# One transfer of 8 KB a partition for each head's position scores, in place of two of 4 KB

## The chip, the cores and the metric

The kernel runs on one core of a Trainium2 chip. The metric is the device time of one execution in microseconds, the median of several runs. The numbers of the profile come from one execution that the hardware profiler recorded.

## What is computed

The input is 32 batches of 512 tokens with 256 channels. A layer norm gives xn. To x are added an attention with relative positions over xn and a mixture of experts over xn. What matters here is the attention, with 16 heads of 16 channels:

```python
content_score = einsum('bhsp,bhtp->bhst', q + u, k)
pos_score = einsum('bhsp,htp->bhst', q + v, pos)
pos_score = _relative_shift(pos_score)      # pad one column in front, reshape (s, s+1) -> (s+1, s), drop the first row
score = (content_score + pos_score) / sqrt(P)
weights = softmax(score, axis=-1)
out = einsum('bhst,bhtp->bhsp', weights, val)
```

There are 32 x 16 = 512 heads, each with 512 x 512 position scores in fp32, 1 MB.

## The kernel before

The kernel has two phases. The attention phase first normalises all batches and then goes through the 512 heads; the expert phase (`ffn_phase`) follows, and begins when the attention phase has ended.

The relative shift of a head is done by memory. A partition holds four query rows. PE computes the position scores of a head into PSUM (`position`, L980), two query tiles at a time. ACT copies these two tiles into a ring of NW = 4 heads, `xo`, with a zero column in front of each row (`x_evacuate`, L604); two copies make a head, and each adds 1 to the semaphore `x_out`. SP writes the ring to the scratch tensor `xs_d` in DRAM as 512 rows of 513 words (`write_x`, L406), and reads the same memory back as rows of 512 words from word 512 on (`read_x`, L416) into `shifted`, which has NX = 8 slots. That is the shifted matrix. Each write and each read is done in two transfers, of rows 0 to 1 and rows 2 to 3 of every partition. Since a partition's four rows lie next to each other, on both sides of each transfer, a transfer of two rows has 4104 or 4096 bytes in one piece per partition, and one of four rows would have 8208 or 8192.

DVE adds the content scores, which PE computes (`content`, L991), to the shifted positions and keeps the least of each row (`add`, L765), then subtracts that least (`subtract_least`, L772). PE turns the result (L1012, L1013), ACT takes the exponential (L612), PE multiplies by the values (L1028). DVE works on head kk, PE and ACT on the positions of head kk + 5 (LEAD = 5).

SP's program is unrolled and strictly in order. In step kk it takes, for half 0 and then half 1: write head kk + 4, read head kk + 2. The waits in it:

- a write waits for the read of the head that had its DRAM slot 8 heads ago (`x_shifted`), and for the ACT copy of its own half (`x_out`);
- a read waits for the whole write of its head, made two steps earlier (`x_written`), and for the slot in `shifted` to be free (`t_full`);
- every fourth step `store_o` issues 4 transfers of 32 KB (L425) and 4 of 2 KB (L428) of finished output; every 16th step a batch's xt is loaded (L368).

ACT waits for `x_written` before it copies into a ring entry again, and DVE waits for `x_shifted` of a head, both halves, before its first addition (L762).

Of the kernel before, what the change touches and what calls it, by code (L numbers as in the profile page):

```python
# [18 lines left out]
B = 32  # L19
S = 512  # L20
TT = S // P
H = 16
# [26 lines left out]
def wait_alone(eng, sem, value):  # L49

    wait(eng, sem, value)
    if not isinstance(value, int):
        eng.nop(nofuse=True)
# [86 lines left out]
def attention_phase(nc, x, gate_w, w, w1, w2, consts, xn_d, xt_d, xs_d, att_d, sums_d, shared):  # L140
# [7 lines left out]
    LEAD = 5  # L148
    BEHIND = 2
    LAG = 2  # L150
    NX = 8
    NW = 4
    ND = 5
    BH = 2 * H
# [6 lines left out]
    with ExitStack() as ctx:  # L161
# [11 lines left out]
        shifted = m.sb("shifted", [P, NX, TT, S])  # L173
# [127 lines left out]
        x_out = m.sem("x_out")  # L301
# [48 lines left out]
        with nc.Block() as block:  # L350

            @block.sync
            def _(sp):
# [42 lines left out]
                        load_xt(0)  # L396
                store_xt(B - 1)

                def write_x(i, kk, half):

                    slot, turn = of_slot(kk)
                    if half == 0:
                        wait_alone(sp, x_shifted[slot], (i * (BH // NX) + turn) * 32)
                    rows = slice(2 * half, 2 * half + 2)
                    wait_alone(sp, x_out, (i * BH + kk) * 2 + half + 1)
                    sp.dma_start(xs_d[slot].rearrange("(p t c) -> p t c", t=TT, c=S + 1)[:, rows], xo[:, kk % NW, rows]).then_inc(x_written[slot], 16)  # L406

                def read_x(i, kk, half):

                    slot, turn = of_slot(kk)  # L410
                    if half == 0:
                        wait_alone(sp, x_written[slot], (i * (BH // NX) + turn + 1) * 32)

                        wait_alone(sp, t_full, (i * BH + kk - NX + 1) * TT)
                    rows = slice(2 * half, 2 * half + 2)
                    sp.dma_start(shifted[:, slot, rows], xs_d[slot][S:S + S * S].rearrange("(p t c) -> p t c", t=TT, c=S)[:, rows]  # L416
                                 ).then_inc(x_shifted[slot], 16)

                def store_o(i, q):

# [12 lines left out]
                for k in range(LEAD - 1):  # L433
                    if k == LEAD - 1 - BEHIND + 1:
                        for n in range(NS):
                            sp.wait_ge(xn_stored[n], 16 * (B // NS))
                            sp.wait_ge(xt_stored[n], 16 * (B // NS))
                    for half in range(2):
                        write_x(0, k, half)
                        if k >= BEHIND:  # L440
                            read_x(0, k - BEHIND, half)
                load_xt(1)

                def body(i):
                    first = isinstance(i, int) and i == 0
                    last = isinstance(i, int) and i == ITERS - 1
                    for kk in range(BH):
                        for half in range(2):
                            if not (last and kk + LEAD - 1 >= BH):
                                write_x(i, kk + LEAD - 1, half)  # L450
                            if not (last and kk + LEAD - 1 - BEHIND >= BH):
                                read_x(i, kk + LEAD - 1 - BEHIND, half)
                        if kk % H == 4 and not last:
                            load_xt(i * 2 + 2 + kk // H)
                        if kk % QH == 0 and not (first and kk < 2 * QH):
                            store_o(i, kk // QH - 2)
                        if last and kk == BH - 2:

                            for k in range(NX):
                                sp.wait_ge(x_written[k], B * H // NX * 32)  # L460
                            load_first(sp, w1, 0, w1s).then_inc(shared.w1_in, 16)
                            load_second(sp, w2, 0, w2s).then_inc(shared.w2_in, 16)

# [80 lines left out]
            def _(act):  # L544
# [53 lines left out]
                def x_evacuate(i, kk, half):  # L598

                    if half == 0 and not (isinstance(i, int) and i * BH + kk < NW):  # L600
                        slot, turn = of_slot(kk - NW)
                        act.wait_ge(x_written[slot], (i * (BH // NX) + turn + 1) * 32)
                    act.wait_ge(x_full, (i * BH + kk) * 2 + half + 1)
                    act.activation(xo[:, kk % NW, 2 * half:2 * half + 2, 1:S + 1], xp[:, :, :], ACT.Copy).then_inc(x_out, 1)  # L604

# [79 lines left out]
            def _(dve):  # L685
# [72 lines left out]
                def add(i, kk, t):  # L758

                    n = i * BH + kk  # L760
                    if t == 0:
                        slot, turn = of_slot(kk)  # L762
                        wait_alone(dve, x_shifted[slot], (i * (BH // NX) + turn + 1) * 32)
                    wait_alone(dve, s_full, n * TT + t + 1)
                    dve.tensor_tensor_reduce(out=shifted[:, kk % NX, t], in0=sp_[:, t % 2], in1=shifted[:, kk % NX, t], scale=-0.25,  # L765
                                             scalar=-NEG, op0=ALU.add, op1=ALU.min,
                                             accum_out=mn[:, kk % NX, t:t + 1]).then_inc(added, 1)
# [895 lines left out]
```

## Time and profile before

| | before |
|---|---|
| time, median of 3 runs | 4691.83 us (4685.78 to 4698.15) |
| profiled execution | 4698.8 us, span 4697.0 us |
| PE busy | 4317.0 us, 92% of the span |
| DVE busy | 3394.8 us, 72% |
| ACT busy | 3201.7 us, 68% |
| POOL busy | 1263.8 us, 27% |
| moved by DMA | 1391.15 MB, mean 296 GB/s |

Busy shares are averages over two phases with different limits: the heads are written and read from 160 to 3047 us, and the experts follow. Where time is lost is read from the waits of a stage and from the share of the 16 DMA engines in it. The profile's DMA share of a stretch is the time of the packets in it over 16 engines; as the records of neighbouring packets overlap a little, it can stand slightly above 1. A PE that is busy isn't PE at its peak, since matmuls are pipelined and their ends are modelled.

### The profile page before, as it was taken

The numbers are of one execution on the slowest core, as the hardware profiler recorded it, in microseconds if no ns is written. First come the engines' busy times: TensorE is split into PE (matmuls) and PEld (weight loads), VectorE is DVE, ScalarE is ACT, GpSimd is POOL, SyncE is SP. The second block draws the span as 40 slices with busy tenths as digits, with TensorE's granted clock in tenths as the row PEclk, the third lists the DMA queues.
The fourth block names the chain that finished last, engine by engine and source line by source line (L and its number), as shares of the span: only waits on it lengthen the run. The fifth ranks groups of instructions, "written<-read, shape, count | busy, mean of one in ns | idle before, by whom it ended". The sixth has DMA issues, their size and how long they took to land. (4 is left out here: it accounts for less than half of the span.)

```text
span 4697.0 us, 121317 instructions
## 1 busy us (share of the span) xinstructions
PE 4317.0 (92%) x48308; PEld 3333.7 (71%) x48308; DVE 3394.8 (72%) x8088; ACT 3201.7 (68%) x4124; POOL 1263.8 (27%) x905
## 2 busy tenths in 40 slices
PE   7899999999989999989998998889999999999997
PEld 3466666666666666666666666668888888888886
DVE  7688888888888888888888787755665666544455
ACT  2588888888888888888888888744444444444454
POOL 0111111111111111111111111125556666544443
PEclk9899999999999999999999999989999999999998
DMA  8999999999999999999999999972555555433259
GB/s 320 342 379 389 394 386 393 388 384 392 389 389 384 388 396 389 388 396 382 390 389 387 391 393 388 360 253 53 133 137 124 136 125 136 107 56 87 47 171 313
DMA packets 467836, 1391.15 MB, mean 296 GB/s; under 512 B 59216, under 2 KB 136656, under 8 KB 467024
## 3 DMA queue, kind: packets, MB, share of 16 engines
q1 hardware_dynamic: 418128, 1316.25, 74.1%
q0 software_dynamic: 49152, 67.14, 8.4%
q8 instruction: 391, 6.41, 0.5%
q14 instruction: 165, 1.35, 0.1%
HBM read 708.93 MB, written 674.23 MB: 294 GB/s over the span
## 5 line engine op out<-in xcount | busy, mean ns | idle before, releaser
L765 DVE CUSTOM_DVE_ANT_0 att_shifted<-att_quad,att_shifted 128x512 f32<-128x512 f32 x2048 | 1351.8, 686 | 507.4 <-PE att_quad L991 256.2
L604 ACT ACTIVATE ring<-att_quad 128x1024 f32<-128x1024 f32 x1024 | 1050.5, 1026 | 229.9 <-PE att_quad L980 205.2
L612 ACT ACTIVATE att_pt<-att_tp 128x1024 f32<-128x1024 f32 x1024 | 1047.7, 1023 | 17.9 <-PE att_tp L1013 13.0
L772 DVE TENSOR_SCALAR att_shifted<-att_shifted,att_mn 128x512 f32<-128x512 f32 x2048 | 1024.6, 542 | 0.0
L991 PE MATMUL att_quad<-att_kd,att_qd 64*128 64x512 f32 x2048 | 879.8, 462 | 149.2 <-DVE att_mn L765 134.6
L980 PE MATMUL att_quad<-att_pos,att_qd 64*128 64x512 f32 x2048 | 849.8, 445 | 91.4 <-ACT ring L604 84.1
L1420 ACT ACTIVATE ffn_hp<-ffn_up 128x512 fp32r<-128x512 f32 x512 | 306.2, 598 | 855.4 <-PE ffn_up L1601 818.4
L1506 DVE TENSOR_TENSOR ffn_hp<-ring,ffn_hp 128x512 fp32r<-128x512 f32 x512 | 440.4, 860 | 589.4 <-ACT ring L1422 528.8
L1012 PEld LDWEIGHTS att_tp<-ident,att_shifted 64*128 64x128 f32 x8192 | 669.6, 141 | 189.2 <-DVE att_shifted L772 109.9
L1601 PE MATMUL ffn_up<-ffn_xp,ffn_w1p 128*128 128x512 f32 x3072 | 796.1, 395 | 2.8 <-DVE ffn_xp L1449 2.8
L1012 PE MATMUL att_tp<-ident,att_shifted 64*128 64x64 f32 x8192 | 754.8, 229 | 43.1 <-ACT att_pt L612 32.8
L1013 PE MATMUL att_tp<-ident,att_shifted 64*128 64x64 f32 x8192 | 762.4, 230 | 2.5 <-issue 2.5
L1559 PE MATMUL ffn_yp<-ffn_w2p,ffn_hp 128*128 128x512 f32 x2048 | 745.5, 398 | 8.7 <-DVE ring L1465 6.9
L1013 PEld LDWEIGHTS att_tp<-ident,att_shifted 64*128 64x128 f32 x8192 | 669.3, 141 | 41.8 <-issue 6.1
L1601 PEld LDWEIGHTS ffn_up<-ffn_xp,ffn_w1p 128*128 128x128 f32 x3072 | 543.4, 189 | 115.9 <-DVE ffn_xp L1449 3.2
L991 PEld LDWEIGHTS att_quad<-att_kd,att_qd 64*128 64x128 f32 x2048 | 377.4, 190 | 334.3 <-DVE att_mn L765 217.9
L1351 POOL DMA_INDIRECT ffn_d<-ring,picks x256 | 432.0, 1688 | 634.8 <-DVE ring L1465 618.5
L1028 PE MATMUL att_op<-att_pt,att_val 128*17 128x128 f32 x16384 | 588.1, 286 | 8.3 <-issue 7.7
L1561 PE MATMUL ffn_yp<-ffn_w2p,ffn_hp 128*128 128x256 f32 x2048 | 573.7, 280 | 0.0
L980 PEld LDWEIGHTS att_quad<-att_pos,att_qd 64*128 64x128 f32 x2048 | 364.5, 190 | 199.5 <-issue 169.2
L499 POOL CAST att_kc<-att_qn 128x512 fp32r<-128x512 f32 x64 | 41.5, 648 | 1584.9 <-PE att_mp L910 1572.8
L1028 PEld LDWEIGHTS att_op<-att_pt,att_val 128*17 128x17 f32 x16384 | 422.5, 101 | 57.5 <-issue 10.0
(132 smaller groups left out, 5249.9 us busy)
## 6 DMA issues: line engine op xcount, KB each, us to landing
xs_d<-ring SPq DMA_DIRECT2D x1024, 513.0 KB, 8.7
att_shifted<-xs_d SPq DMA_DIRECT2D x1024, 512.0 KB, 8.8
att_shifted<-in_L_attn_x_dram SPq DMA_DIRECT2D x32, 512.0 KB, 6.6
xn_d<-att_shifted SPq DMA_DIRECT2D x32, 512.0 KB, 5.9
xt_d<-att_shifted SPq DMA_DIRECT2D x32, 512.0 KB, 7.2
gathered<-xt_d SPq DMA_DIRECT2D x32, 512.0 KB, 10.0
att_d<-att_osb SPq DMA_DIRECT2D x512, 32.0 KB
ring<-in_L_ffn_w_dram SPq DMA_DIRECT2D x16, 1024.0 KB
```

The source lines that it names most:

```text
L604: act.activation(xo[:, kk % NW, 2 * half:2 * half + 2, 1:S + 1], xp[:, :, :], ACT.Copy).then_inc(x_out, 1)
L612: act.activation(turned_keys(n, half), tp[:, :, :].rearrange("p r (k n) -> p k r n", k=2 * TT), ACT.Exp, scale=-1.0).then_inc(t_out, 1)
L765: dve.tensor_tensor_reduce(out=shifted[:, kk % NX, t], in0=sp_[:, t % 2], in1=shifted[:, kk % NX, t], scale=-0.25, scalar=-NEG, op0=ALU.ad ...
L772: dve.tensor_scalar(shifted[:, kk % NX, t], shifted[:, kk % NX, t], mn[:, kk % NX, t:t + 1], None, ALU.subtract).then_inc(lowered, 1)
L980: ins = pe.matmul(xp[:, t % 2, :], qd[rows, n // GH % ND, t * P:(t + 1) * P], pos[rows, kk // GH % NG8, :], start=True, stop=True)
L991: pe.matmul(sp_[:, t % 2, :], qd[rows, n // GH % ND, t * P:(t + 1) * P], kd[rows, kk // GH % 2, :], start=True, stop=True).then_inc(s_full, 1)
L1012: low = pe.transpose(tp[:, 0, at], shifted[0:ROWS, kk % NX, t, keys], ident[0:ROWS, 0:ROWS])
L1013: high = pe.transpose(tp[:, 1, at], shifted[ROWS:P, kk % NX, t, keys], ident[ROWS:P, ROWS:P])
L1028: ins = pe.matmul(op[32 * t:32 * t + HD + 1, kk % QH * P:(kk % QH + 1) * P], val[:, kk // H % 2, c, kk % H, :], pt[:, of_keys(n, c), t * P ...
L1559: pe.matmul(yp[:, k % 2, :], hp[:, g % 2, 0, f, tok], w2p[:, f].rearrange("p w d -> p (w d)"), start=(f == 0), stop=False)
L1561: ins = pe.matmul(yp[:, k % 2, 0:D], hp[:, g % 2, 1, f, tok], w2p[:, f, 0], start=False, stop=(f == FC - 1))
L1601: ins = pe.matmul(up[:, f % 4, :], w1p[:, wi, c, f * P:(f + 1) * P], xp[:, g % 2, xi, c, :], start=(s == 0 and c == 0), stop=(s == 2 and c ...
```

## The change

`write_x` and `read_x` lose their argument `half`. A head is written by one transfer of all four rows of a partition, once both ACT copies are done, and read by one. SP's order in step kk is now: write head kk + 4, read head kk + 2. The semaphores `x_written` and `x_shifted` go up by 16 a head in place of 32, and all that wait for them are adapted. The bytes, the buffers, the distances between heads and the other engines' programs are as before.

```diff
-                def write_x(i, kk, half):
+                def write_x(i, kk):
 
                     slot, turn = of_slot(kk)
-                    if half == 0:
-                        wait_alone(sp, x_shifted[slot], (i * (BH // NX) + turn) * 32)
-                    rows = slice(2 * half, 2 * half + 2)
-                    wait_alone(sp, x_out, (i * BH + kk) * 2 + half + 1)
-                    sp.dma_start(xs_d[slot].rearrange("(p t c) -> p t c", t=TT, c=S + 1)[:, rows], xo[:, kk % NW, rows]).then_inc(x_written[slot], 16)
-
-                def read_x(i, kk, half):
+                    wait_alone(sp, x_shifted[slot], (i * (BH // NX) + turn) * 16)
+                    wait_alone(sp, x_out, (i * BH + kk) * 2 + 2)
+                    sp.dma_start(xs_d[slot].rearrange("(p t c) -> p t c", t=TT, c=S + 1), xo[:, kk % NW]).then_inc(x_written[slot], 16)
+
+                def read_x(i, kk):
 
                     slot, turn = of_slot(kk)
-                    if half == 0:
-                        wait_alone(sp, x_written[slot], (i * (BH // NX) + turn + 1) * 32)
-
-                        wait_alone(sp, t_full, (i * BH + kk - NX + 1) * TT)
-                    rows = slice(2 * half, 2 * half + 2)
-                    sp.dma_start(shifted[:, slot, rows], xs_d[slot][S:S + S * S].rearrange("(p t c) -> p t c", t=TT, c=S)[:, rows]
-                                 ).then_inc(x_shifted[slot], 16)
+                    wait_alone(sp, x_written[slot], (i * (BH // NX) + turn + 1) * 16)
+
+                    wait_alone(sp, t_full, (i * BH + kk - NX + 1) * TT)
+                    sp.dma_start(shifted[:, slot], xs_d[slot][S:S + S * S].rearrange("(p t c) -> p t c", t=TT, c=S)).then_inc(x_shifted[slot], 16)
...
-                        for half in range(2):
-                            if not (last and kk + LEAD - 1 >= BH):
-                                write_x(i, kk + LEAD - 1, half)
-                            if not (last and kk + LEAD - 1 - BEHIND >= BH):
-                                read_x(i, kk + LEAD - 1 - BEHIND, half)
+                        if not (last and kk + LEAD - 1 >= BH):
+                            write_x(i, kk + LEAD - 1)
+                        if not (last and kk + LEAD - 1 - BEHIND >= BH):
+                            read_x(i, kk + LEAD - 1 - BEHIND)
```

## Rows read from the trace of the kernel before

**Rows 1.** The page: DMA share and GB/s in 40 slices of the span, SP's queue.

```profile
DMA  8999999999999999999999999972555555433259
GB/s 320 342 379 389 394 386 393 388 384 392 389 389 384 388 396 389 388 396 382 390 389 387 391 393 388 360 253 53 133 137 124 136 125 136 107 56 87 47 171 313
...
q1 hardware_dynamic: 418128, 1316.25, 74.1%
```

**Rows 2.** The page: issues of the positions' transfers, count, KB each, us to landing.

```profile
xs_d<-ring SPq DMA_DIRECT2D x1024, 513.0 KB, 8.7
att_shifted<-xs_d SPq DMA_DIRECT2D x1024, 512.0 KB, 8.8
```

**Rows 3.** Stages: busy time of each engine, granted clock, DMA share and rate.

```profile
core 0: us, PE busy (x) PEld busy (x) DVE busy (x) ACT busy (x) POOL busy (x), PEclk, DMA share, GB/s
...
1000.00:1500.00 500.00, 452.18 (x6858) 334.02 (x6858) 414.89 (x1122) 424.54 (x491) 71.77 (x56) 0.97 1.01 389
```

**Rows 4.** Waits of the whole span, the last two SP's own.

```profile
engine line waited for: us in total, times, longest us
...
DVE att_shifted L765 <- PE att_quad L991: 256.2, 376, 2.8
DVE att_shifted L765 <- DMA att_shifted<-xs_d: 236.7, 276, 2.3
...
SPq L406 <- ACT ring L604: 448.2, 386, 9.7
...
SPq L416 <- DMA xs_d<-ring: 284.2, 241, 3.4
```

**Rows 5.** The queues in 2064 to 2070, 1518 to 1521, 2034 to 2036 us.

```profile
DMA packets 675, 2.47 MB, mean 412 GB/s; under 512 B 73, under 2 KB 73, under 8 KB 674
...
q1 hardware_dynamic: 674, 2.46, 102.3%
...
DMA packets 539, 0.97 MB, mean 323 GB/s; under 512 B 99, under 2 KB 335, under 8 KB 538
...
q1 hardware_dynamic: 538, 0.95, 85.2%
...
DMA packets 418, 0.71 MB, mean 354 GB/s; under 512 B 80, under 2 KB 269, under 8 KB 418
...
q1 hardware_dynamic: 418, 0.71, 102.5%
```

**Rows 6.** The sums' load in SP's timeline, and the queue from 3079 to 3081 us.

```profile
3076.62 0.35 SPq L1254 DMA_DIRECT2D ffn_heads<-sums_d  x1
...
DMA packets 97, 0.74 MB, mean 369 GB/s; under 512 B 5, under 2 KB 5, under 8 KB 9
...
q1 hardware_dynamic: 97, 0.74, 100.8%
```

**Rows 7.** SP's timeline around a quad's stores: start, duration, line, transfer.

```profile
1514.75 0.43 SPq L416 DMA_DIRECT2D att_shifted<-xs_d  x1
1515.22 2.23 SPq L425 DMA_DIRECT2D att_d<-att_osb  x4
1517.49 2.39 SPq L428 DMA_DIRECT2D sums_d<-att_osb  x4
1519.97 0.39 SPq L406 DMA_DIRECT2D xs_d<-ring  x1
1520.46 0.38 SPq L416 DMA_DIRECT2D att_shifted<-xs_d  x1
1520.89 0.78 SPq L406 DMA_DIRECT2D xs_d<-ring  x1
1521.71 0.51 SPq L416 DMA_DIRECT2D att_shifted<-xs_d  x1
...
1525.02 0.32 SPq L406 DMA_DIRECT2D xs_d<-ring  x1
...
1527.66 0.32 SPq L406 DMA_DIRECT2D xs_d<-ring  x1
...
1530.16 0.32 SPq L406 DMA_DIRECT2D xs_d<-ring  x1
```

**Rows 8.** Line L406, the writes: from issue to landing.

```profile
DMA to landing us min/median/max: 3.3/8.7/10.9
```

More of the change, by code:

```diff
@@ L437, in _ @@
                             sp.wait_ge(xt_stored[n], 16 * (B // NS))
-                    for half in range(2):
-                        write_x(0, k, half)
-                        if k >= BEHIND:
-                            read_x(0, k - BEHIND, half)
+                    write_x(0, k)
+                    if k >= BEHIND:
+                        read_x(0, k - BEHIND)
                 load_xt(1)
@@ L447, in body @@
                     for kk in range(BH):
-                        for half in range(2):
-                            if not (last and kk + LEAD - 1 >= BH):
-                                write_x(i, kk + LEAD - 1, half)
-                            if not (last and kk + LEAD - 1 - BEHIND >= BH):
-                                read_x(i, kk + LEAD - 1 - BEHIND, half)
+                        if not (last and kk + LEAD - 1 >= BH):
+                            write_x(i, kk + LEAD - 1)
+                        if not (last and kk + LEAD - 1 - BEHIND >= BH):
+                            read_x(i, kk + LEAD - 1 - BEHIND)
                         if kk % H == 4 and not last:
@@ L459, in body @@
                             for k in range(NX):
-                                sp.wait_ge(x_written[k], B * H // NX * 32)
+                                sp.wait_ge(x_written[k], B * H // NX * 16)
                             load_first(sp, w1, 0, w1s).then_inc(shared.w1_in, 16)
@@ L601, in x_evacuate @@
                         slot, turn = of_slot(kk - NW)
-                        act.wait_ge(x_written[slot], (i * (BH // NX) + turn + 1) * 32)
+                        act.wait_ge(x_written[slot], (i * (BH // NX) + turn + 1) * 16)
                     act.wait_ge(x_full, (i * BH + kk) * 2 + half + 1)
@@ L762, in add @@
                         slot, turn = of_slot(kk)
-                        wait_alone(dve, x_shifted[slot], (i * (BH // NX) + turn + 1) * 32)
+                        wait_alone(dve, x_shifted[slot], (i * (BH // NX) + turn + 1) * 16)
                     wait_alone(dve, s_full, n * TT + t + 1)
```

## The prediction

> **What bounds the kernel now.** The page comes first. Its slices show two stages: up to about 3050 us DMA stands at 9 in every slice and moves 340 to 396 GB/s; behind that it falls to 40 to 140 GB/s for most of the rest [rows 1]. The change touches the first stage only. The 2048 half transfers of the positions [rows 2] carry 2048 x 512.5 KB, 1075 of the 1316 MB of SP's queue [rows 1].
>
> Next the stage table: from 1000 to 1500 us PE is busy 452, ACT 425 and DVE 415 of 500 us, the clock is granted at 0.97, and the DMA engines have a share of 1.01 at 389 GB/s [rows 3]. (A share above 1 says that the times of neighbouring packets overlap a little in the records.) So DMA has no room left; PE, ACT and DVE have 10, 15 and 17%.
>
> The waits say the same from the other side [rows 4]. DVE waits 236.7 us for a shifted head to land, in 276 of 512 heads, and 256.2 us for PE's content scores. SP waits 284.2 us for a write to land before it may read it back. PE's waits on DVE follow from these. So the loop is held by the DMA engines, with PE near behind. Full DMA engines mean that the time of a head is the work that those engines have for it: cut the work per head, and the loop gets shorter, until PE is next.
>
> **What a transfer costs on the engines.** The change leaves the bytes as they are and halves the number of packets, so I need the fixed cost of a packet. Three short stretches of the queue view give it [rows 5]. The first holds big transfers alone: 674 packets, 2.46 MB, 102.3% of 16 engines x 6 us = 98.2 us of packet time. The second holds many small ones: 538 packets, 0.95 MB, 85.2% of 48 us = 40.9 us. With time = n x o + bytes x b, the second scaled by 2.46 / 0.95 = 2.589 is 1393 packets and 105.9 us for the same bytes; the difference is 719 packets for 7.7 us, so o = 10.7 ns. The third (418 packets, 0.71 MB, 102.5% of 32 us = 32.8 us), scaled by 3.465, gives 774 packets for 15.4 us, o = 19.9 ns. The two differ by 9 ns, so I take 1.5 to 20 ns as bounds and 10.7 as the value: a wait inside a packet can only make o look larger.
>
> In the first stretch 73 packets are under 512 B and 601 are not, 8.2 to 1: each half transfer is 128 packets of 4 KB (one a partition) and 16 small closing ones.
>
> **The change, part by part.**
>
> 1. *Half the packets.* 2048 transfers of 144 packets become 1024 of 144, if 8 KB of a partition go in one packet. That they can is shown by the one transfer of before with 8 KB a partition, the sums' load at 3076.62 us: its stretch has 97 packets of which 9 are under 8 KB [rows 6]. 147,456 packets fewer, 9216 on each of 16 engines, x 10.7 ns = 98.6 us. It counts only where the engines are full: heads are moved from slice 2 to slice 26, and 23 of these 25 stand at 379 GB/s or more [rows 1], so 0.92 x 98.6 = 91 us. By the bounds: 13 to 169 us (1.5 and 20 ns).
>
> 2. *The first half of a write waits for the second.* A write now waits for both ACT copies of its head. Where no stores lie between, write halves go out at 1525.02, 1527.66 and 1530.16, 2.5 us apart [rows 7]. What is queued behind the waiting SP: the read of two heads earlier, and every fourth head the 8 small stores. Before, the read's first half went ahead of that wait, but DVE starts a head only when both halves have landed, so its last byte is issued at the same moment as before. The engines lose nothing as long as they have over 3 us of work queued at that time. From issue to landing a half transfer takes 8.7 us in the median [rows 8], and carries 1.3 us of work at 411 GB/s; the shortest, 3.3 us, is one with next to nothing ahead of it. So 5 us or more lie ahead in the median, which covers the wait: cost nothing. If that cover were gone it would be up to 1.3 us a head.
>
> 3. *The write is whole before the read of its turn.* On the engines the order was write half, read half, write half, read half; now write, then read. A write lands one half transfer (1.3 us) sooner relative to what is queued, and it is the write two heads ago for which SP waits 284.2 us before reading [rows 4]. That wait shrinks. I book nothing, since the engines were not idle during it.
>
> 4. *SP's issue.* Two issues a head in place of four, 0.32 us each when nothing is in the way. Every fourth head SP issues the stores of a quad, 1515.22 to 1519.88, and no large transfer goes out [rows 7]; then it catches up with issues of 0.4 to 0.8 us each, one behind the other. The engines pause after that: the q1 share of 85.2% over 3 us is a pause of 0.44 us [rows 5]. 128 such groups make at most 56 us. With whole transfers SP hands over twice the bytes an issue, so part of this may be won; I put it in the range, not in the sum. The waits' thresholds (16 in place of 32) cost nothing: the same number of waits, or fewer.
>
> 5. *What is late next.* The 91 us are 0.18 us of a head's 5.59 us (two issues of each kind a head, 1024 in all over 2870 us). DVE's landing waits are 0.46 us a head, so more is there than is taken. PE at 452 of 500 us still has room for a period shorter by 3.2%.
>
> Sum: 4697.0 us span plus 1.8 around it is 4698.8 us for the profiled execution; less 91 is 4608. That execution is 7 us above the median of the three runs, so against the median: 4601 us.
>
> **A rule of the notes that speaks against it.** The Trainium skill (DMA: Bandwidth & Descriptors, "Why small descriptors are slow (HBM only)") puts the fixed overhead at about 3 cycles a packet and holds joining to be worth it only at 256 B or less. With the 850 MHz that the page gives for the fabric that would be an estimate of 3.5 ns a packet, 9216 x 3.5 = 32 us, a time near 4660. The stretches above gave 10.7 and 19.9 ns, but they are few.
>
> **The rivals.**
>
> *B, the packet's fixed cost is small, or PE takes over at once.* At the low end of my bounds, 1.5 to 4 ns, part 1 is worth 13 to 34 us: 4658 to 4679, take 4670. The same time results if PE gives only a third of what DMA frees: DVE waits for PE more than for DMA [rows 4]. Against it: the engines show shares of 1.00 and more nearly throughout.
>
> *C, slower: the held first half starves the engines.* Place: the head behind a quad's stores, where the queue has run down. If the engines stand for one half transfer there, 1.3 us x 128 groups = 166 us, less the 91 us: +75, 4767 us. It decides from the point where less than about 3 us of work is queued when a first half becomes ready. For it: the 3.3 us shortest landing and the pauses in [rows 5]. Against: after the stores both halves are ready already, as the four issues from 1519.97 on without a gap show [rows 7].
>
> *D, slower: 8 KB packets take longer.* The stretch with the 8 KB load has 88 large packets and 9 others in 100.8% of 32 us, 32.3 us; all of it laid on the large ones is up to 367 ns each [rows 6]. In the plain stretch two 4 KB packets take 2 x 98.2 / 601 = 327 ns with their closing packets. If 367 held, 40 ns x 8192 large packets an engine = +328 us, 5020 us; the point from which it loses is 327 ns. I give this little, because that stretch holds the start of an idle queue, with the first packets' latency in it.
>
> *E, the change doesn't do what it says: the 8208 B rows of the write are cut into a large packet and a remainder.* Then only the reads have fewer packets: half of part 1, -46 us, 4646 us.
>
> **How the numbers follow.** A, my sum: 0.57, with its own range 4570 to 4640 (10.7 ns, give or take a third, and a part of the pauses). A with the pauses gone or a packet cost of 20 ns, some 4545 us: 0.07. B 0.14, C 0.10, D 0.05, E 0.07. A measurement of this kernel tells 0.3%, 14 us, from no change. Faster: A, its better case, E and about a third of B, 0.75; same: the rest of B, 0.10; slower: C and D, 0.15. The range runs from 4550 to 4690: it leaves out C and D (0.15) and about 0.05 at the low end.
>
> **What would show it.** Step 1: packets of q1 down by 147,456 to some 271,000, and plain stretches at 420 GB/s or more in place of 410. Step 2: no new pauses of DMA between quads, DVE's landing waits below 236.7 us; if they grow while the DMA share drops below 0.97, C is right. Step 3: SP's waits for written heads well below 284.2 us. Step 4: shares after the stores above 85%. Step 5: PE's busy share in the stage up from 0.90 to about 0.93. Wrong would be the sum if plain stretches stay at 410 GB/s (B or D), or if they rise and the period of a head doesn't fall below 5.5 us (PE next).

## The result, and the profile after

The changed kernel takes 4848.65 us (median of 4 runs, 4837.81 to 4869.45), the kernel before 4688.81 us on the same chip: a ratio of 1.034, 95% interval 1.032 to 1.036. It is slower by 160 us, where 90 us less was forecast. The profiled execution has a span of 4867.6 us.

| | before | after |
|---|---|---|
| span of the profiled execution | 4697.0 us | 4867.6 us |
| packets of SP's queue | 418128 | 270672 |
| DMA rate, 1000 to 1500 us | 389 GB/s | 361 GB/s |
| PE's granted clock, same stretch | 0.97 | 0.94 |
| DVE waits for a shifted head | 236.7 us | 339.8 us |

The page of the kernel after, in the form of [rows 1] and [rows 2]:

```profile
DMA  9899999999999999999999999984445555433259
GB/s 331 319 364 362 350 378 370 370 364 354 361 370 371 357 374 380 357 359 374 372 362 365 371 365 368 369 325 127 111 114 140 136 125 138 115 63 84 45 158 314
...
q1 hardware_dynamic: 270672, 1316.18, 74.9%
...
xs_d<-ring SPq DMA_DIRECT2D x512, 1026.0 KB, 8.5
att_shifted<-xs_d SPq DMA_DIRECT2D x512, 1024.0 KB, 10.6
```

The queue has exactly the 147,456 packets fewer that were forecast, for the same bytes, and yet its share of the span is no smaller. In the stage of the heads the slices stand at 350 to 380 GB/s where they stood at 379 to 396, and the stage lasts longer by that. The stage behind it is as it was. (The granted clock of PE goes along with this and doesn't look like its cause: PE is busy for less of the stretch, 437 us in place of 452, though its clock is lower.) The table of stages, to be held against [rows 3], and the waits of the whole span, against [rows 4] (SP's own last):

```profile
1000.00:1500.00 500.00, 436.81 (x6413) 321.36 (x6408) 388.90 (x1046) 395.81 (x458) 65.81 (x52) 0.94 1.00 361
...
DVE att_shifted L758 <- DMA att_shifted<-xs_d: 339.8, 301, 5.0
...
DVE att_shifted L758 <- PE att_quad L984: 322.5, 369, 3.2
...
SPq L46 <- ACT ring L597: 1783.5, 398, 9.8
```

SP's wait for the landing of a write, 284.2 us before, is down to 2.6 us. In its place SP stands 1783.5 us in the wait for both ACT copies (L46 is the helper `wait_alone`). Before, its waits for ACT copies were 448.2 us [rows 4] and, counted at the same helper, 349.3:

```profile
SPq L46 <- ACT ring L604: 349.3, 262, 3.9
```

The DMA share still reads 1.00 while the rate fell by 7%: the engines are counted busy with packets that move fewer bytes in the same time, as if they stood still for a part of it. Over the whole span this can be put in numbers. The share of q1, SP's queue, times the span is the time that its packets took on each engine: 74.1% of 4697.0 us is 3481 us before, 74.9% of 4867.6 us is 3646 us after. A third fewer packets for the same bytes took 165 us more, and what is left of the span grew only from 1216 to 1222 us. So the changed kernel isn't longer because its engines are idle more; its packets are slower.

Where packets stand still is seen in 1 us windows (columns as in [rows 3]: the last two are DMA share and GB/s), with SP's issues of that time:

```profile
1500.10 0.32 SPq L404 DMA_DIRECT2D xs_d<-ring  x1
1500.51 0.38 SPq L412 DMA_DIRECT2D att_shifted<-xs_d  x1
1505.28 0.32 SPq L404 DMA_DIRECT2D xs_d<-ring  x1
1505.69 0.38 SPq L412 DMA_DIRECT2D att_shifted<-xs_d  x1
1506.12 2.31 SPq L420 DMA_DIRECT2D att_d<-att_osb  x4
...
1505.00:1506.00 1.00, 1.00 (x6) 0.66 (x4) 0.59 (x1) 1.00 (x2) 0.00 (x0) 1.00 1.02 419
1506.00:1507.00 1.00, 1.00 (x15) 0.71 (x16) 1.00 (x5) 0.81 (x2) 0.00 (x0) 1.00 1.14 320
1507.00:1508.00 1.00, 1.00 (x42) 0.93 (x40) 1.00 (x2) 0.98 (x2) 0.00 (x0) 1.00 0.89 262
1508.00:1509.00 1.00, 1.00 (x20) 0.70 (x9) 1.00 (x5) 0.95 (x2) 0.00 (x0) 1.00 0.96 402
1509.00:1510.00 1.00, 1.00 (x20) 0.90 (x18) 1.00 (x3) 0.85 (x2) 0.81 (x1) 1.00 1.05 443
```

The engines are at 419 GB/s, drop to 320 and 262 for 2 us with shares of 1.14 and 0.89, and come back. A quad's stores are issued from 1506.12 on and may have a part in this one, but it returns about once a head, after each whole write: 324 and 321 GB/s from 1512 to 1514 us, and, where no store is near, 246 and 254 from 1500 to 1502 and 295 from 1518 to 1519. The plain stretch of before from 2064 to 2070 us stayed at 394 to 422 GB/s in each microsecond, 412 in the mean [rows 5].

### The profile page after: what moved, and what is told of

It is laid out like the page before. It is cut to its first block and busy times, and to the rows that moved or that the text cites. A ratio compares the mean times of both kernels' runs of the same rounds, so it can differ in the third digit from the quotient of the medians.

```text
span 4867.6 us, 120293 instructions
## 1 busy us (share of the span) xinstructions
PE 4397.3 (90%) x48308; PEld 3383.3 (70%) x48308; DVE 3408.2 (70%) x8088; ACT 3203.3 (66%) x4124; POOL 1243.2 (26%) x905
## 3 DMA queue, kind: packets, MB, share of 16 engines
q1 hardware_dynamic: 270672, 1316.18, 74.9%
## 5 line engine op out<-in xcount | busy, mean ns | idle before, releaser
L758 DVE CUSTOM_DVE_ANT_0 att_shifted<-att_quad,att_shifted 128x512 f32<-128x512 f32 x2048 | 1353.3, 685 | 669.3 <-DMA att_shifted<-xs_d 339.8
L984 PE MATMUL att_quad<-att_kd,att_qd 64*128 64x512 f32 x2048 | 903.5, 472 | 248.9 <-DVE att_mn L758 234.5
L973 PE MATMUL att_quad<-att_pos,att_qd 64*128 64x512 f32 x2048 | 882.6, 457 | 86.5 <-ACT ring L597 79.5
L1499 DVE TENSOR_TENSOR ffn_hp<-ring,ffn_hp 128x512 fp32r<-128x512 f32 x512 | 452.4, 884 | 571.3 <-ACT ring L1415 571.2
L1005 PE MATMUL att_tp<-ident,att_shifted 64*128 64x64 f32 x8192 | 774.9, 233 | 41.1 <-ACT att_pt L605 28.2
L1005 PEld LDWEIGHTS att_tp<-ident,att_shifted 64*128 64x128 f32 x8192 | 690.9, 144 | 171.5 <-DVE att_shifted L765 90.9
L1006 PE MATMUL att_tp<-ident,att_shifted 64*128 64x64 f32 x8192 | 779.3, 233 | 0.3 <-issue 0.2
L1006 PEld LDWEIGHTS att_tp<-ident,att_shifted 64*128 64x128 f32 x8192 | 690.7, 144 | 51.3 <-issue 13.1
L984 PEld LDWEIGHTS att_quad<-att_kd,att_qd 64*128 64x128 f32 x2048 | 388.9, 195 | 450.2 <-DVE att_mn L758 334.0
L1021 PE MATMUL att_op<-att_pt,att_val 128*17 128x128 f32 x16384 | 626.9, 299 | 9.9 <-issue 9.2
L973 PEld LDWEIGHTS att_quad<-att_pos,att_qd 64*128 64x128 f32 x2048 | 375.6, 194 | 190.8 <-issue 158.8
L1021 PEld LDWEIGHTS att_op<-att_pt,att_val 128*17 128x17 f32 x16384 | 440.6, 105 | 74.3 <-issue 11.8
```

Source lines behind the costliest of these rows:

```text
L973: ins = pe.matmul(xp[:, t % 2, :], qd[rows, n // GH % ND, t * P:(t + 1) * P], pos[rows, kk // GH % NG8, :], start=True, stop=True)
L984: pe.matmul(sp_[:, t % 2, :], qd[rows, n // GH % ND, t * P:(t + 1) * P], kd[rows, kk // GH % 2, :], start=True, stop=True).then_inc(s_full, 1)
L1005: low = pe.transpose(tp[:, 0, at], shifted[0:ROWS, kk % NX, t, keys], ident[0:ROWS, 0:ROWS])
L1006: high = pe.transpose(tp[:, 1, at], shifted[ROWS:P, kk % NX, t, keys], ident[ROWS:P, ROWS:P])
L1021: ins = pe.matmul(op[32 * t:32 * t + HD + 1, kk % QH * P:(kk % QH + 1) * P], val[:, kk // H % 2, c, kk % H, :], pt[:, of_keys(n, c), t * P ...
```

## The experiments

Three theories stood at the start. **P**: 8 KB packets make the engines stall. **O**: long stretches of one direction do, a whole write and then a whole read, in place of halves by turns. **H**: the write's first half, held back until both copies are there, costs the time. A fourth, **L**, came with the third group: every transfer issued later lands later, and the heads are tied to the landing. The times are medians, the ratios are to the kernel before on the same chip.

### One part of the change at a time

**by_partitions** keeps write, read, write, read, but halves a head by partitions, with 8 KB packets:

```diff
-                    rows = slice(2 * half, 2 * half + 2)
-                    wait_alone(sp, x_out, (i * BH + kk) * 2 + half + 1)
-                    sp.dma_start(xs_d[slot]...[:, rows], xo[:, kk % NW, rows])
+                    part = slice(64 * half, 64 * half + 64)
+                    wait_alone(sp, x_out, (i * BH + kk) * 2 + 2)
+                    sp.dma_start(xs_d[slot]...[part], xo[part, kk % NW])
...
```

> A head is still moved by two writes and two reads in the order write, read, write, read, but the halves are partitions 0 to 63 and 64 to 127, so that every packet is 8 KB; all of them wait for both ACT copies. If 8 KB packets make the engines stall (theory P), it is as slow as the changed kernel, 4830 to 4870 us. If it is the order, a whole write and then a whole read (theory O), 8 KB packets cost nothing and save their fixed cost: 4590 to 4650 us. If it is the first half held back (theory H), 4770 to 4850 us.

Measured: 5460.63 us, ratio 1.165 (1.163 to 1.167). Far outside all three. The rate of its stage is 308 GB/s:

```profile
1000.00:1500.00 500.00, 396.29 (x5402) 288.82 (x5399) 328.32 (x881) 335.50 (x389) 59.28 (x46) 0.86 1.00 308
```

The edit brought a cost of its own and tells nothing on P, O and H. It is taken up again with the transfers alone.

**order_wwrr** changes the order of the four transfers to write, write, read, read, and nothing else:

```diff
...
                         for half in range(2):
                             if not (last and kk + LEAD - 1 >= BH):
                                 write_x(i, kk + LEAD - 1, half)
+                        for half in range(2):
                             if not (last and kk + LEAD - 1 - BEHIND >= BH):
```

> The kernel before with its four transfers a head, 4 KB packets and waits, but issued write, write, read, read. P: as before, 4670 to 4710 us. O: as slow as the changed kernel or more, 4830 to 4950 us (long packets where the engines go from writes to reads). H: as before, since the first write half still goes out on its own copy.

Measured: 4768.63 us, 1.016 (1.014 to 1.018). Between the two, outside all three ranges: the order costs, but only half of what O asked for. The edit isn't O alone, because the read's first half is now also behind the second copy.

**first_half_held** changes one number:

```diff
-                    wait_alone(sp, x_out, (i * BH + kk) * 2 + half + 1)
+                    wait_alone(sp, x_out, (i * BH + kk) * 2 + 2)
```

> The kernel before in every way but one: the first write half waits for both ACT copies. H: 4770 to 4850 us. P and O: as before, 4680 to 4720 us.

Measured: 4841.16 us, 1.032 (1.030 to 1.035). This hits H in full: with 4 KB packets, four transfers and the old order, the hold alone costs 150 us. That is nearly the changed kernel's 160, but it isn't yet the same loss, as the packets' times below show.

**quarters** is by_partitions with 32 partitions at a time:

> As by_partitions with quarters of 32 partitions, 8 KB packets, write and read by turns, 256 KB each, 8 issues a head of 0.32 us or more. P: 4830 to 4870 us. O: no slower than by_partitions, 4580 to 4650 us, unless SP's eight issues a head (2.6 us at least of 5.5) hold it up after the stores.

Measured: 5481.86 us, 1.170 (1.167 to 1.173), like by_partitions and as far outside its ranges.

### Reads in front

If the hold costs because reads stand behind it, reads issued first should be free of it. **read_first_whole** turns the changed kernel's two issues round, **read_first_halves** makes the same of before, read, read, write, write:

```diff
+                        if not (last and kk + LEAD - 1 - BEHIND >= BH):
+                            read_x(i, kk + LEAD - 1 - BEHIND)
                         if not (last and kk + LEAD - 1 >= BH):
                             write_x(i, kk + LEAD - 1)
-                        if not (last and kk + LEAD - 1 - BEHIND >= BH):
-                            read_x(i, kk + LEAD - 1 - BEHIND)
```

> The changed kernel with SP's order in a step turned round: read head kk + 2 whole, then write head kk + 4 whole, so that no read stands behind an ACT copy of its own step. If the loss comes from reads that are issued only behind the second copy (theory H), it goes: 4620 to 4700 us, with DVE's waits for landings under those of the changed kernel by half. If it comes from 8 KB packets or from a whole write followed by a whole read (P, O), it stays: 4800 to 4870 us.

> The kernel before with the order read, read, write, write, 4 KB packets. H: a little better than before, 4620 to 4690 us, as its second read half no longer waits for the second copy. O (long stretches of one direction cost): like order_wwrr, 4740 to 4790 us. The difference to read_first_whole is the packet size and the first write half's hold: P expects read_first_whole slower by 60 us or more, H within 40 us.

Measured: 4851.99 us, 1.035 (1.032 to 1.037), and 4846.17 us, 1.033 (1.031 to 1.035). H in this form falls: the read no longer stands behind a copy, and nothing is won. What SP stands before now is shown by its waits in read_first_whole from 1000 to 2000 us, 611.8 us for written heads to land, and the write queues behind that:

```profile
SPq L412 <- DMA xs_d<-ring: 611.8, 146, 7.1
```

That this wait is what costs the time is not shown. The packets of both kernels took longer than before's (3667 and 3678 us an engine against 3481) and the rest of the span is shorter (1183 and 1168 us against 1216), so the engines didn't idle for want of issues; and the order read, write is slow with whole transfers without any computation too (358 GB/s, below).

**read_whole** (write half, write half, read whole) and **write_whole_between** (read half, write whole, read half) mix the sizes:

> Writes by halves as before, each on its own copy, then the read whole (8 KB packets): write, write, read. Against order_wwrr (4769 us, same order and same waits, 4 KB reads) only the read's packets and one issue change. Packets' fixed cost alone: 40 to 50 us less, 4720 to 4735 us; P (8 KB packets stall): 4800 us or more.

> Write whole (8 KB packets), read by halves of rows around it: read half, write, read half. The first read half no longer waits for any copy, the second for both, as before. H: 4680 to 4760 us, between before and the changed kernel, since less is issued at the second copy. P: 4760 to 4830 us for the writes' packets. O: 4740 to 4800 us.

Measured: 4757.33 us, 1.016 (1.013 to 1.019), and 4796.95 us, 1.024 (1.021 to 1.027). Whole reads in place of two halves, at the same order and the same waits, are no slower than order_wwrr (ratios of 1.016 both, on two chips, with intervals that overlap): P fails for reads, and of the 40 to 50 us that the packets were to bring, 11 at most arrive. write_whole_between, in which SP holds the whole write and the second read half, lies in the ranges of P and O and above that of H, and doesn't part P from O.

### The distance between write and read

**behind_one_whole** and **behind_one_halves** read a head one step behind its write:

```diff
-    BEHIND = 2
+    BEHIND = 1
...
```

> The changed kernel with each head read one step behind its write in place of two (read head kk + 3 in step kk), so that a read has a head's time more until DVE needs it, while SP waits longer for the write to land. L: the loop has more room, 4700 to 4800 us. P, O: the engines' time is what it was, 4830 to 4870 us. Slower than the changed kernel, 4900 us or more, if SP's wait for the fresh write delays the next write by more than it brings.

> The kernel before with the same single edit, reads one step behind the writes. L: 4620 to 4700 us. Slower than before, 4750 us or more, if the wait for the fresh write holds back the second write half.

Measured: 4990.05 us, 1.063 (1.061 to 1.065), and 5407.76 us, 1.152 (1.150 to 1.154). L falls; the other branch came true, and by far. In behind_one_whole SP stands 635.2 us from 1000 to 2000 us before writes that have yet to land. That this wait costs the time is argued: the DMA share stays at 1.01 there while the rate is 351 GB/s, and only in behind_one_halves does it fall, to 0.94 at 310 GB/s (500 to 2500 us).

### Transfers alone

**transfers_alone** leaves the computation out. SP moves 40 heads in each of nine ways, and a write waits for the read four heads earlier, so that about as much is in flight as in the kernel (row halves land after 7.9 us for writes and 8.5 for reads in the median, where the kernel before has 8.7 and 8.8):

```python
for k in range(HEADS):
    wait_read(k - 4)
    for part in parts:
        write(k, part)
        if k >= 2:
            if part[1] == 0:
                wait_write(k - 2)
            read(k - 2, part)
```

> No computation at all (the output is x): SP alone moves 40 heads' positions in each of nine ways, one after the other, a write waiting for the read of four heads earlier to land, a read for its own write, issued two heads earlier. It measures what each pattern costs the DMA engines with nothing else in the loop. If 8 KB packets or long stretches of one direction cost the engines time (P, O), write and read whole moves fewer GB/s than by row halves by turns, by 5% or more, with packets that take over 340 ns in the mean. If the loss needs the loop (theory L: every transfer that is issued later lands later, and the heads are tied to the landing), whole transfers move 3% more, 415 to 425 GB/s against 405 to 412. Halves by partitions should stay near 310 GB/s, since their packets took twice as long in the kernel too.

The windows of the nine ways (no engine works but DMA; the last two columns are DMA share and GB/s), in this order: row halves by turns; row halves write, write, read, read; whole, write then read; whole, read then write; partition halves by turns; writes only in row halves, writes only whole; reads only in row halves, reads only whole:

```profile
23.00:202.00 179.00, 0.00 (x0) 1.00 1.03 409
229.00:412.00 183.00, 0.00 (x0) 1.00 1.03 401
439.00:629.00 190.00, 0.00 (x0) 1.00 1.01 384
656.00:861.00 205.00, 0.00 (x0) 1.00 1.01 358
888.00:1125.00 237.00, 0.00 (x0) 1.00 1.01 318
1152.00:1254.00 102.00, 0.00 (x0) 1.00 1.00 333
1281.00:1380.00 99.00, 0.00 (x0) 1.00 0.97 341
1407.00:1486.00 79.00, 0.00 (x0) 1.00 1.03 410
1513.00:1588.00 75.00, 0.00 (x0) 1.00 1.01 422
```

Four things stand in these rows. Whole transfers, write then read, run at 384 GB/s against 409 for row halves by turns: the change loses 6% of the rate with no loop around it, and L, which wanted 415 to 425, falls. The 384 is the mean of a rate that wanders: in windows of 10 us it is 321 to 341 GB/s from 450 to 480 us and 393 to 417 from 490 to 590. Reads alone gain the packets' cost, 410 to 422. Writes alone have 333 and 341 GB/s in the mean, so the 409 of the mixture rests on reads running beside them. And partition halves are at 318, near the 308 of by_partitions: its slow rate comes with the transfers and not from the loop. Each of these ways ran once.

The reads-only windows also give the packet's cost without any stall in the way:

```profile
q1 hardware_dynamic: 8888, 32.35, 102.7%
...
q1 hardware_dynamic: 4341, 31.63, 101.3%
```

The first has 102.7% of 16 x 79 us, 1298 us, the second 101.3% of 16 x 75 us, 1216 us. Scaled to 32.35 MB the second is 4440 packets and 1243 us; 4448 packets fewer for 55 us is 12.3 ns each.

**transfers_alone_2** adds halves of even and of odd partitions, `xo[half::2]`: 8 KB packets, half a head a transfer, spread over all partitions.

> Transfers alone again (no computation, the output is x), 40 heads each in nine ways, with halves of even and of odd partitions, which have 8 KB packets and yet go over the whole of the partitions. Long stretches are the cause (O): even and odd halves by turns reach 415 to 425 GB/s, the same halves as write, write, read, read fall to 385 to 400, near whole transfers (383). Packets are the cause (P): even and odd halves by turns stay under 395 GB/s. Single rows of 2 KB by turns, short stretches with twice the packets: 380 to 392 GB/s by their fixed cost. Mixed (writes by 4 KB rows, reads by even and odd): 412 to 418 by O.

The windows, in this order: row halves by turns; even and odd by turns; writes by rows and reads by even and odd, by turns; even and odd as write, write, read, read; row halves as write, write, read, read; whole, write then read; single rows of 2 KB by turns (the two left, whole writes then row-half reads and row-half writes then whole reads, have 370 and 392 GB/s):

```profile
23.00:202.00 179.00, 0.00 (x0) 1.00 1.03 408
229.00:400.00 171.00, 0.00 (x0) 1.00 1.01 422
427.00:604.00 177.00, 0.00 (x0) 1.00 1.02 414
631.00:805.00 174.00, 0.00 (x0) 1.00 1.01 418
832.00:1021.00 189.00, 0.00 (x0) 1.00 1.04 387
1048.00:1248.00 200.00, 0.00 (x0) 1.00 1.01 364
1275.00:1508.00 233.00, 0.00 (x0) 1.00 1.02 324
```

8 KB packets by turns move 422 GB/s, 3.5% more than 4 KB ones: P falls. But O falls too in its plain form, because even and odd halves as write, write, read, read have stretches as long as whole transfers and 8 KB packets as well, and keep 418, where 385 to 400 was expected. What slows whole transfers (364 here, 384 in the first run), and row halves in that order (387 and 401), is neither the packet nor the length of the stretch by itself; what it is, these runs don't tell. Single rows of 2 KB move 324 GB/s where 380 to 392 was expected, so a fixed cost a packet doesn't foretell a mixture either. Each way ran once here too, and the two runs differ by 4 and 5% in the two slow ways, so only the larger gaps count.

**held_even_odd** and **reads_even_odd** bring these halves into the kernel, the first for writes and reads and with both copies waited for, the second only for the reads, whose edit is shown:

```diff
-                    rows = slice(2 * half, 2 * half + 2)
-                    sp.dma_start(shifted[:, slot, rows], xs_d[slot]...[:, rows])
+                    part = slice(half, P, 2)
+                    sp.dma_start(shifted[part, slot], xs_d[slot]...[part])
```

> first_half_held (4841 us) with halves of even and odd partitions in place of row halves: same order, same waits, same number of issues, but 8 KB packets for writes and reads. O: the packets save their fixed cost and nothing else changes, 4760 to 4810 us. P: as slow as the changed kernel or slower, 4850 to 4920 us.

> The kernel before with its order, waits and writes, but with the reads by even and odd partitions: 8 KB packets in the reads, no write held back, and no stretch of one direction longer than before. O and L: half of the packets' gain without either cost, 4640 to 4680 us. P: 4700 to 4780 us.

Measured: 4963.75 us, 1.059 (1.057 to 1.061), and 4675.86 us, 0.997 (0.995 to 0.998). The second lies in the range of O and L and is a little faster than before, by 16 us, a third of the 46 that half of the packets were to bring. The first contradicts everything expected: the pattern that is fastest alone is 123 us slower than first_half_held with the same waits. The stages from 500 to 2500 us of first_half_held and held_even_odd show what it lacks:

```profile
500.00:2500.00 2000.00, 1765.13 (x26079) 1298.38 (x26080) 1579.68 (x4248) 1614.58 (x1864) 270.63 (x213) 0.94 0.99 370
...
500.00:2500.00 2000.00, 1732.17 (x25043) 1272.74 (x25041) 1530.48 (x4080) 1551.33 (x1791) 262.30 (x206) 0.91 0.94 355
```

A DMA share of 0.99 and 0.94, where before has 1.01: in the held kernels the engines are idle for a part of the time. One place is behind a quad's stores. SP's timeline of first_half_held, and the windows of the same time:

```profile
1655.19 0.94 SPq L406 DMA_DIRECT2D xs_d<-ring  x1
1656.18 0.72 SPq L416 DMA_DIRECT2D att_shifted<-xs_d  x1
1656.94 2.81 SPq L425 DMA_DIRECT2D att_d<-att_osb  x4
1659.79 2.38 SPq L428 DMA_DIRECT2D sums_d<-att_osb  x4
1662.29 0.38 SPq L406 DMA_DIRECT2D xs_d<-ring  x1
...
1660.00:1662.00 2.00, 1.72 (x35) 1.28 (x39) 2.00 (x9) 1.97 (x3) 0.00 (x0) 1.00 0.98 387
1662.00:1664.00 2.00, 2.00 (x42) 1.51 (x30) 1.42 (x5) 1.41 (x2) 0.00 (x0) 1.00 0.72 259
1664.00:1666.00 2.00, 2.00 (x26) 1.88 (x24) 1.53 (x6) 2.00 (x3) 0.00 (x0) 1.00 0.91 158
1666.00:1668.00 2.00, 2.00 (x50) 1.72 (x52) 1.81 (x4) 1.07 (x3) 0.00 (x0) 1.00 0.86 287
```

For 6 us the engines move 259, 158 and 287 GB/s. Below 410 GB/s that is (151 + 252 + 123) x 2 us = 1.05 MB, a whole write of lost work, 2.6 us, behind one quad's stores. It is one of the deeper cases, and before has such a dip as well (307, 184 and 363 GB/s from 1520 to 1526 us, behind the stores of [rows 7]). What the hold adds is seen only over many quads. The mean rate in GB/s of the 82 to 90 quads between 500 and 2500 us, in windows of 2 us that start so many us after the first store's issue:

| window starts at | -4 | -2 | 0 | 2 | 4 | 6 | 8 | 10 | 12 | a quad takes |
|---|---|---|---|---|---|---|---|---|---|---|
| before | 412 | 404 | 406 | 409 | 363 | 337 | 311 | 406 | 410 | 22.39 us |
| first_half_held | 404 | 390 | 343 | 398 | 347 | 306 | 246 | 373 | 404 | 23.60 us |
| held_even_odd | 397 | 352 | 292 | 404 | 274 | 259 | 196 | 387 | 412 | 24.59 us |
| the changed kernel | 393 | 348 | 377 | 366 | 349 | 369 | 366 | 332 | 364 | 23.80 us |

From -2 to 14 us first_half_held moves 0.48 MB less than before, 1.17 us of work at 410 GB/s, and its quad is 1.21 us longer: nearly all of its loss lies around the stores. The changed kernel's loss doesn't. Behind the stores, from 4 to 10 us, it moves more than before (361 GB/s in the mean against 337), and less in every other window.

### The stores spread

That gives a test: if the hold costs at this one place, it costs nothing once SP is never away for 5 us. The stores of a quad are spread over four steps, one of 32 KB and one of 2 KB each, in four kernels: before, first_half_held, the changed kernel, reads_even_odd.

```diff
-                        if kk % QH == 0 and not (first and kk < 2 * QH):
-                            store_o(i, kk // QH - 2)
+                        if not (first and kk < 2 * QH):
+                            store_o(i, kk // QH - 2, (kk % QH,))
```

> The kernel before with a quad's eight small stores spread: one of 32 KB and one of 2 KB in each of the four steps, in place of all eight in every fourth step, so that SP is never away for 4.7 us. The pauses behind the stores go: 4600 to 4680 us. If the small transfers' own time on the engines is what costs there, no change: 4680 to 4710 us.

> The same spreading in first_half_held (4841 us: row halves by turns, first write half behind both copies). If the hold costs because the queue runs dry behind the stores, most of its 150 us goes: within 50 us of stores_spread. If it costs in every head, it stays 100 us or more above stores_spread.

> The same spreading in the changed kernel (4849 us). If whole writes and whole reads cost the engines what they did alone (383 GB/s or less against 409), 4740 to 4850 us, clearly above held_stores_spread. If the hold behind the stores was all, within 30 us of held_stores_spread or below it by the packets' 90 us.

> reads_even_odd (4676 us) with the stores spread: no hold, turns as before, 8 KB packets in the reads, no pause behind the stores. 10 to 30 us below stores_spread: 4580 to 4660 us.

| | stores together | stores spread |
|---|---|---|
| row halves, as before | 4688.81 to 4694.96 | 4686.80, ratio 1.000 (0.999 to 1.001) |
| first half held | 4841.16 | 4691.13, 1.000 (0.999 to 1.001) |
| whole transfers (the change) | 4848.65 | 4747.63, 1.012 (1.010 to 1.015) |
| reads by even and odd | 4675.86 | 4669.54, 0.995 (0.994 to 0.997) |

The hold's 150 us go to 4 us, within the noise. Before itself gains nothing from the spreading, where 4600 to 4680 us was expected: taking its pauses of [rows 5] away wins nothing, and the other branch (4680 to 4710, the small transfers' own time) is the one that fits. The changed kernel keeps 57 us over held_stores_spread, as the first branch had it, which is what whole transfers cost beside the hold. The stages from 500 to 2500 us of held_stores_spread and whole_stores_spread:

```profile
500.00:2500.00 2000.00, 1810.34 (x27488) 1336.17 (x27489) 1652.75 (x4477) 1697.65 (x1964) 282.96 (x222) 0.97 1.01 389
...
500.00:2500.00 2000.00, 1783.61 (x26906) 1311.48 (x26908) 1627.85 (x4383) 1661.86 (x1923) 278.04 (x220) 0.97 1.01 381
```

The held kernel is back at the 389 GB/s of [rows 3], the whole transfers stay at 381. even_odd_stores_spread is the fastest kernel of this study, 0.5% under before; it is 17 us under stores_spread as expected, but above its range of 4580 to 4660, which counted on a gain from the spreading.

How long SP's packets took on each engine (q1's share times the span), and what is left of the span, parts two kinds of loss, slower packets and idle engines (roughly, since neighbouring packets overlap a little in the records):

| | packets, us | rest of the span, us |
|---|---|---|
| before | 3481 | 1216 |
| first_half_held | 3560 | 1283 |
| the changed kernel | 3646 | 1222 |
| order_wwrr | 3601 | 1175 |
| held_stores_spread | 3489 | 1200 |
| whole_stores_spread | 3536 | 1210 |

The hold alone costs both: 79 us of slower packets and 67 us of idle engines. The changed kernel and the changed order cost slower packets alone.

## Why the prediction was wrong, point by point

*What bounds the kernel.* Right: each kernel that moved fewer GB/s in the stage took longer. But "DMA has no room left" was taken to mean that the work per head is bytes and packets and nothing else. A share of 1 says that the engines have packets, not how fast these move: it stood beside 389 GB/s before and beside 361 after.

*Step 1, the packets.* The count was right to the packet. The cost was near: 12.3 ns for reads alone where 10.7 was taken, with some luck, since the two short stretches gave 10.7 and 19.9. The Trainium skill's figure (DMA: Bandwidth & Descriptors, "Why small descriptors are slow (HBM only)"), from which the prediction worked out an estimate of 3.5 ns, is well below the 12.3 measured here, which is all that a packet adds, whatever its parts. The failure is the silent half of the step, that the bytes' part stays what it is. The step forecast 99 us less of packets' time on each engine, and the changed kernel has 165 us more. Whole transfers alone move 384 GB/s in place of 409; in the kernel this is 57 us with the stores spread, net of what the packets save.

*Step 2, the held first half.* This is the other step that failed: "5 us or more lie ahead in the median, which covers the wait: cost nothing". Taken alone, the hold cost 150 us. A median over all heads says nothing about the head where the queue is shortest, and around the stores it costs 1.17 us a quad. Rival C named this place and nearly this price, 1.3 us x 128 groups = 166 us, and gave it 0.10, because "after the stores both halves are ready already". For first_half_held C is right; that 166 is so near to 150 is in part luck, since only 67 us of it are idle engines. For the changed kernel C's own sign didn't come: DVE's landing waits grew, from 236.7 to 339.8 us, but the DMA share stayed at 1.00 where below 0.97 was asked for, and what is left of the span beside the packets' time hardly grew, from 1216 to 1222 us. There the loss is slower packets, in all parts of a quad. It depends on the stores even so, since spreading them gives back 101 us.

*Step 3, the write lands sooner.* SP's wait for written heads did go, from 284.2 to 2.6 us. It was no gain: SP waits for the copies in its place.

*Step 4, SP's issue.* Its sign came true, and no time was won by it. Behind the stores the changed kernel moves 361 GB/s in the mean where before has 337, with shares of 0.99 to 1.04. Before gained nothing from having its pauses taken away either.

*Step 5* never came to bear. PE's busy share in the stage fell to 0.87.

*Rival D*, given 0.05, said that 8 KB packets take longer, and that above 327 ns for a large packet with its closing part the change loses. It is nearest to what the changed kernel's own trace shows: 165 us more of packets' time on an engine, half of D's 328. For whole transfers alone its limit is passed: 10001 packets of which 1113 are small, 101.1% of 16 x 190 us, 3073 us over 8888, 346 ns.

```profile
DMA packets 10001, 72.89 MB, mean 384 GB/s; under 512 B 1113, under 2 KB 1113, under 8 KB 1113
...
q1 hardware_dynamic: 10001, 72.89, 101.1%
```

But 8 KB isn't the reason: by the same sum even and odd halves by turns take 315 ns (8808 large packets of 11008 in 101.4% of 16 x 171 us).

*Rivals B and E* fell: the packets' cost is real where reads run alone, and no row was cut, as the count of packets shows.

How the 160 us add up is shown in two ways by the table of the spread stores: hold first, 150, then whole, 8; or with the stores spread, hold 4, then whole 57, with 101 for the stores' place. So the parts of the change that cost are the hold and the whole transfers, and both cost more beside stores that are issued together. They overlap, and the sum has no single split.

**Left open.** Why a transfer of all 128 partitions, or row halves in the order write, write, read, read, makes packets slower, when even and odd halves in that order don't. Why stores that are issued together slow the changed kernel's packets in all parts of a quad. Why held_even_odd is slower than first_half_held: that its engines idle more is shown (1407 us of its span are free of SP's packets, 1283 in first_half_held), that faster transfers empty the queue sooner is only argued. And the saving of reads_even_odd, 16 us of 46, was not followed further.

## What to carry to other kernels

A queue that is full on average has an emptiest moment, here behind eight small issues in a row, and that is where a wait added to the issuing engine's program cost: read the rate in 2 us windows through that place, over many turns and beside the same windows of the kernel before, and not the median time to landing. Ask also whether a loss is idle engines or slower packets: the queue's share times the span tells them apart, and a price for a packet taken from one pattern need not hold in another. Before transfers are joined, ask what of them could go out earlier than the last part of their source, and which other direction runs beside them. Where a join is wanted for its packets, try another split that keeps the turns: halves of every second partition, for the reads alone, brought 0.3% here and 0.5% with the stores spread, while for reads and writes with both copies waited for they lost 5.9%.

## What the runs showed of the hardware

- Without computation, writes to DRAM alone ran at 333 to 341 GB/s, reads alone at 410 to 422, and halves of both by turns (row halves, even and odd) at 408 to 422. Such a mixture was as fast as reads alone.
- Half a head by partitions 0 to 63 and 64 to 127 moves 318 GB/s, by even and odd partitions 422, with packets of the same sizes and counts. The Trainium skill (DMA: Bandwidth & Descriptors, "Rules for kernel authors") says of two transfers to disjoint partition halves "Don't bother — they serialize"; here contiguous halves were a sixth slower than one transfer of all (384), and interleaved ones a tenth faster (16% against the 364 of their own run). The same section wants 1 MiB or more a transfer for most bandwidth; the 1 MB transfers here were slower in the mixture (364 to 384 GB/s) than 0.5 MB ones by turns (408 to 422), and faster only where one direction ran alone (422 against 410 for reads, 341 against 333 for writes).
- A DMA share near 1 isn't full use: in 1 us windows of the kernel after 320 GB/s stood beside a share of 1.14 and 443 beside 1.05, and from 1000 to 1500 us 361 GB/s beside 1.00, where before has 389 beside 1.01.
